# Two attention layers on one core: the last head group is normalised with its channels in rows, and the instruction lists are reordered

## The chip, the cores and the metric

The kernel runs on one core of a Trainium2 chip. The metric is the time of one execution on the device, in microseconds (us). TensorE (PE) multiplies and transposes, VectorE (DVE) and ScalarE (ACT) work on tiles, GpSimd (POOL) prepares tables and small tiles, SyncE (SP) issues DMAs. "Ln" is line n of the kernel.

## What is computed

A map `x` of 16 x 16 positions with 192 channels goes through two layers, each `x = x + attention(groupnorm(x))`:

```python
def _gn(v, G=32, eps=1e-05): ...           # mean and variance over positions and 6 channels
q, k, v = proj(x)                          # 12 heads of 16 channels, 256 tokens
attn = (q * scale) @ k.T                   # per head, 256 x 256
attn = attn + rel_h[..., :, None] + rel_w[..., None, :]   # from q and tables of 31 x 16
out = softmax(attn) @ v
return out @ wo + bo
```

The second layer adds low-rank parts to its q and v weights. Everything is float32.

## The kernel before, in words

The kernel is one hand-written list of instructions for each engine, with a semaphore wait ahead of every step that needs another engine's result. The order on an engine is the order of its list; no scheduler changes it. Both layers run the same lists. The 192 channels are held as two chunks of 96 rows; 12 heads are three groups (g) of four, or six pairs (p).

**Start.** SP loads `x`, then for each layer the input weights `win` and the output weights `wout` (three DMAs: 128 rows, 64 rows, the bias row). PE runs matmuls on a zero tile (`keep_busy`, L587) whose result nobody reads: 23 at the start, 3 between the two matmul groups that sum the statistics (`group_records`, L598 and L601), 12 before the projections of layer 0. DVE computes the statistics (L513, L517, L523), POOL the inverse deviation (L229), DVE the normalised input `xn` (L533).

**Projections and moves.** PE projects q and k (`project`, L785) and v (`values`, L775); ACT and DVE split q and k into a rounded and a rest part (`zq`, `zk`, `z_hi` and `z_lo`). `relative` (L804, four quarters) makes the position terms, which ACT rounds (`relative_rounded`) and DVE completes (`relative_rest`, L482). `key_rows` (L627), `query_rows` (L641) and `relative_rows` (L658) spread a group over PSUM banks, and 18 "moves" (`ACT_MOVES`, 12, and `DVE_MOVES`, 6; kind, group, odd or even heads) copy them to `ks` and `qs`. Kind k, q or r names which of the three it is. Group 0 and 1 share banks, so the spread of the next group waits for the moves of the one before it.

**Scores.** For each pair, `scores` (L672) makes scores with the queries in rows, DVE takes each row's maximum (`maxima`, L476), POOL splits it (`split_maxima`), PE turns it (`turn_max`, L686), ACT writes it beside the queries (`max_rows`). `scores_t` (L700) makes the scores again with the keys in rows, less the maximum, and ACT takes the exponential of a pair (`probabilities`, L382) or, for the last pair, of half a pair at a time (`last_probabilities`, L388). `max_rows` and `move` share one helper line, L335, on ACT.

**End of a layer.** `probs_v` (L719) multiplies the probabilities of a group by `va`, which holds for each head 16 value columns, a column of ones and 15 of zeros, so the product of a group has 128 rows: per head 16 channels, the softmax sum, 15 zeros. In each group it is copied to `ot` (DVE for groups 0 and 1, `out_columns`, L488; ACT for group 2), turned to tokens in rows (`turn_out`, L729), normalised by a reciprocal of the 8 sums of a row and a product (`normalise`, L467 and L469) into `on`, and turned back (`turn_on`, L736, first channels 0 to 127, then the remaining 64), and ACT copies each to `ont`. `residual` (L744, L749) puts `x` into the output banks and `output_product` (L757 in layer 0, L760 in layer 1) adds the product with `wout`: first both halves m of chunk 0, then both of chunk 1, whose extra row of ones brings the bias. In layer 0, DVE's next statistics wait for each half; in layer 1, ACT and DVE copy out the result and it is stored.

The list of PE at the end of a layer:

```python
scores_t(l, 4, 0); scores_t(l, 4, 1)
turn_out(l, 0)
scores_t(l, 5, 0); scores_t(l, 5, 1)
probs_v(l, 1); probs_v(l, 2)
turn_out(l, 1); residual(l, 1); turn_out(l, 2)
turn_on(l, 0); residual(l, 0); turn_on(l, 1)
```

Of the kernel before, what the change touches and what calls it, by code (L numbers as in the profile page):

```python
# [12 lines left out]
P = 128  # L13
# [20 lines left out]
def attention_layers(nc, x, w_in0, w_out0, w_in1, w_out1, lora, rel, out):  # L34
# [4 lines left out]
    with ctx:  # L39
# [3 lines left out]
        def sem(name):  # L43
# [52 lines left out]
        rinv = sb("rinv", [P, NG, TT, G4])  # L96
        on = sb("on", [P, TT, C])
# [32 lines left out]
        rstd_sb = sem("rstd_sb")  # L130
        lora_zero, lora_sb = sem("lora_zero"), sem("lora_sb")
# [11 lines left out]
        O_BANK, NM_BANK = [2, 2, 5], 3  # L143
        ONT_BANK = [3, 2]
# [10 lines left out]
        ON_ROWS = [P, C - P]  # L155
# [68 lines left out]
        def _(pool):  # L224
# [67 lines left out]
            pool.wait_ge(parts_hi, 1)  # L292
            spread_steps(0, 0)
# [39 lines left out]
        def _(act):  # L333
# [63 lines left out]
            for l in range(LAYERS):  # L397
# [37 lines left out]
        def _(dve):  # L435
# [3 lines left out]
            dve.memset(xn[CH:CH + 1, 0, :], 1.0).then_inc(made_ones, 1)  # L439
            dve.memset(ont[C - P:C - P + 1, 1, :], 1.0).then_inc(made_ones, 1)  # L440
            dve.memset(onehot[:, :, :], 0.0).then_inc(key_rows_sb, 1)
            dve.memset(pick_rh[:, :, 0:2].bitcast(F32), 0.0).then_inc(pick_zero, 1)
            dve.memset(pick_rh[:, :, 33:64].bitcast(F32), 0.0).then_inc(pick_zero, 1)
            dve.memset(pick_rl[:, :, 0:33].bitcast(F32), 0.0).then_inc(pick_zero, 1)
            dve.wait_ge(key_rows_sb, 1)
            dve.memset(onehot[64:66, :, :], 1.0).then_inc(key_rows_sb, 1)
            dve.wait_ge(made_ident, 1)
            dve.tensor_reduce(head_mask[:, :], ident[:, :].rearrange("p (s j c) -> p j s c", s=2, j=G4),
                              AX.XY, ALU.add).then_inc(made_mask, 1)
# [7 lines left out]

            def move(l, n):
# [4 lines left out]
            def normalise(l, g):  # L463

                dve.wait_ge(oq_ps, NG * l + g + 1)
                q = ps[:, O_BANK[g], T:2 * T].rearrange("p (t j d) -> p t j d", t=TT, j=G4)
                dve.reciprocal(rinv[:, g, :, :], q[:, :, :, D]).then_inc(ri_sb, 1)  # L467
                dve.wait_ge(ri_sb, NG * l + g + 1)
# [35 lines left out]
            for l in range(LAYERS):  # L504

                for ic in range(NC):
# [7 lines left out]
                    if l == 0 and ic == 0:  # L514
# [5 lines left out]
                                      ALU.mult).then_inc(spread_sb, 1)  # L520
                for ic in range(NC):
                    dve.wait_ge(gn_ps, NC * l + ic + 1)
                    dve.bn_aggr(mv[:, l, ic, :], ps[0:CH, GN_BANK[ic], 0:6 * GROUP]).then_inc(mv_sb, 1)  # L523
                    if l == 0 and ic == 0:
                        dve.wait_ge(rels_sb, 1)
                        dve.tensor_tensor(step[:, 0, :, :], *step_args(0), ALU.subtract).then_inc(step_sb, 1)
                dve.wait_ge(mv_sb, NC * l + NC)
# [29 lines left out]
                move(l, 0)  # L557
                move(l, 1)
                relative_rest(l, 0)
                relative_rest(l, 1)  # L560
                move(l, 2)
                relative_rest(l, 2)
# [9 lines left out]
                out_columns(l, 0)  # L572
                normalise(l, 0)
                out_columns(l, 1)
                normalise(l, 1)
                normalise(l, 2)
# [4 lines left out]
        def _(pe):  # L581
# [124 lines left out]
            def probs_v(l, g, tiles=range(TT)):  # L706
# [5 lines left out]
                elif g == 1:  # L712
                    pe.wait_ge(on_sb, NG * l + 1)
# [9 lines left out]
            def turn_out(l, g):  # L723
                if g < 2:
                    pe.wait_ge(ot_sb, 2 * l + g + 1)
                else:
                    pe.wait_ge(ot_act, l + 1)
# [5 lines left out]
            def turn_on(l, kc):  # L733
                pe.wait_ge(on_sb, NG * l + 2 + kc)
                for t in range(TT):
                    last = pe.transpose(ps[0:ON_ROWS[kc], ONT_BANK[kc], t * P:(t + 1) * P],  # L736
                                        on[:, t, kc * P:kc * P + ON_ROWS[kc]], ident[:, :])
# [15 lines left out]
            def output_product(l, kc, m):  # L753

                k = ON_ROWS[kc] + kc
                if l == 0:
                    return mm(ps[0:CH, Y_BANK + m, 0:T], wout[0][0:k, kc, m * CH:(m + 1) * CH],  # L757
# [180 lines left out]
```

## Time and profile before

| | |
|---|---|
| median of 3 runs | 73.58 us (73.19 to 73.86) |
| profiled execution | 74.05 us, of which the span is 72.3 us |
| PE busy | 65.3 us, 90% of the span |
| PE weight loads | 53.5 us, 74% |
| DVE | 48.4 us, 67% |
| ACT | 49.0 us, 68% |
| POOL | 26.5 us, 37% |

The span is the time from the first to the last recorded work. Busy time counts an instruction from its start to its end. Matmuls overlap, so that the distance between their starts, and not the mean duration, is what one costs in a row of them. Layer 0 fills the span to about 38 us, layer 1 the rest.

### The profile page before, as it was taken

To read this page: it belongs to the slowest core of one execution; us is meant where nothing else is said; L and a number is where in the kernel's file an instruction comes from. 1 tells how busy PE (TensorE), PEld (TensorE's weight loads), DVE (VectorE), ACT (ScalarE), POOL (GpSimd) and SP (SyncE) were. 2 spreads that over 40 slices of the span, in tenths; PEclk is the share of its full clock that TensorE was granted. 3 is DMA by queue.
4 is the path that set the end of the run, shared out by engine and by line. 5 is a ranking of instruction groups with operands and counts; after the bars stand their busy time and mean duration, and the time that the engine had idled before them with its cause. 6 is when DMAs were issued, how large, how long until landed. Compare 5 with 4: busy or idle time off the path is not lost.

```text
span 72.3 us, 1550 instructions
## 1 busy us (share of the span) xinstructions
PE 65.3 (90%) x564; PEld 53.5 (74%) x564; DVE 48.4 (67%) x110; ACT 49.0 (68%) x92; POOL 26.5 (37%) x61
## 2 busy tenths in 40 slices
PE   4999999999988999989999698999987998989960
PEld 4889779999965977664679587999956896655640
DVE  3886437899999898222518939899999897223410
ACT  3962056398999999995324057589999999994410
POOL 5755999997013222899901400000022223000000
PEclk9999999999999999999999999999999999999999
DMA  0978300000000000000000000000000000000003
GB/s 1 206 241 257 102 0 0 9 0 0 0 5 0 0 0 0 14 0 0 0 0 0 5 9 0 0 0 0 0 0 0 0 9 0 0 0 0 0 0 109
DMA packets 1575, 1.75 MB, mean 24 GB/s; under 512 B 344, under 2 KB 1178, under 8 KB 1568
## 3 DMA queue, kind: packets, MB, share of 16 engines
q1 hardware_dynamic: 1280, 1.49, 7.5%
q10 hardware_dynamic: 288, 0.16, 0.7%
q8 instruction: 4, 0.07, 0.4%
q14 instruction: 3, 0.02, 0.1%
HBM read 1.46 MB, written 0.20 MB: 23 GB/s over the span
## 4 chain that ended last, share of the span: by engine, by line
PE 62%; ACT 23%; DVE 7%; issue 3%
ACT pt L382 11%; PE ps L804 10%; ACT qs L335 10%; PE ps L785 9%; PE ps L587 6%; PE ps L672 5%; PE ps L719 5%; PE ps L775 3%; PE ps L641 3%; PE ps L658 3%; PE ps L757 3%; PE ps L627 2%; PE ps L760 2%; PE ps L736 2%; PE ps L700 2%
## 5 line engine op out<-in xcount | busy, mean ns | idle before, releaser
L335 ACT ACTIVATE qs<-ps 64x512 fp32r<-64x512 f32 (+1 forms) x30 | 17.7, 589 | 0.9
L476 DVE TENSOR_REDUCE nm<-ps 128x2 f32<-128x512 f32 x24 | 15.5, 687 | 1.2 <-PE ps L672 0.8
L315 POOL CAST nmhl<-nm 128x4 fp32r<-128x4 f32 x12 | 2.2, 187 | 27.0 <-DVE nm L476 27.0
L672 PE MATMUL ps<-ks,qs 128*128 128x256 f32 x48 | 10.4, 306 | 0.9 <-DVE nm L476 0.3
L382 ACT ACTIVATE pt<-ps 128x1024 f32<-128x1024 f32 x10 | 10.3, 1026 | 0.2
L700 PE MATMUL ps<-qs,ks 128*128 128x256 f32 x48 | 9.5, 300 | 0.8 <-ACT qs L335 0.8
L672 PEld LDWEIGHTS ps<-ks,qs 128*128 128x128 f32 x48 | 7.1, 189 | 2.8 <-issue 2.7
L785 PE MATMUL ps<-xn,win 97*128 97x256 f32 (+1 forms) x24 | 7.9, 496 | 0.6 <-DVE xn L533 0.6
L700 PEld LDWEIGHTS ps<-qs,ks 128*128 128x128 f32 x48 | 6.9, 189 | 1.7 <-issue 1.6
L785 PEld LDWEIGHTS ps<-xn,win 97*128 97x128 f32 (+1 forms) x24 | 6.1, 260 | 1.9 <-issue 0.7
L335 ACT ACTIVATE zq<-ps 64x256 fp32r<-64x256 f32 x6 | 2.3, 378 | 7.1 <-PE ps L785 6.9
L719 PE MATMUL ps<-pt,va 128*32 128x256 f32 x96 | 6.1, 384 | 0.0
L335 ACT ACTIVATE rr_hi<-ps 64x384 fp32r<-64x384 f32 x8 | 3.9, 483 | 3.2 <-PE ps L804 3.0
L587 PE MATMUL ps<-busy 128*128 128x128 bf16 x40 | 4.9, 308 | 1.1 <-DVE busy L438 1.1
L488 DVE COPY ot<-ps 128x256 f32<-128x256 f32 x4 | 1.7, 425 | 5.7 <-PE ps L719 5.7
L686 PE MATMUL ps<-ident_r,nmhl 128*2 128x128 f32 x48 | 4.8, 222 | 0.6 <-ACT qs L335 0.6
L587 PEld LDWEIGHTS ps<-busy 128*128 128x128 bf16 x40 | 4.3, 150 | 1.1 <-DVE busy L438 1.1
L555 DVE TENSOR_TENSOR zq<-ps,zq 64x256 fp32r<-64x256 f32 x6 | 2.5, 421 | 3.4 <-ACT zq L335 3.3
L804 PEld LDWEIGHTS ps<-zq,table_w 128*64 128x64 f32 x64 | 4.2, 138 | 0.5 <-DVE zq L555 0.5
L804 PE MATMUL ps<-zq,table_w 128*64 128x48 f32 x64 | 4.4, 218 | 0.2 <-DVE zq L555 0.2
L686 PEld LDWEIGHTS ps<-ident_r,nmhl 128*2 128x2 f32 x48 | 3.0, 83 | 2.1 <-ACT qs L335 1.9
L461 DVE CAST qs<-ps 64x512 fp32r<-64x512 f32 x6 | 4.1, 690 | 0.5 <-PE ps L641 0.4
(105 smaller groups left out, 126.4 us busy)
## 6 DMA issues: line engine op xcount, KB each, us to landing
win<-in_w_in_dram SPq DMA_DIRECT2D x4, 216.0 KB
xt<-in_x_dram SPq DMA_DIRECT2D x2, 96.0 KB, 2.3
wout<-in_w_out_dram SPq DMA_DIRECT2D x2, 96.0 KB
wout<-in_w_out_dram SPq DMA_DIRECT2D x2, 48.0 KB
out_dram<-res ACTq DMA_DIRECT2D x1, 96.0 KB, 1.7
out_dram<-res SPq DMA_DIRECT2D x1, 96.0 KB, 1.7
rel_raw<-in_rel_dram ACTq DMA_DIRECT2D x1, 62.0 KB, 2.5
win<-in_w_in_dram SPq DMA_DIRECT2D x2, 2.2 KB
```

What stands on the lines that cost most here:

```text
L335: return act.activation(dst, src, ACT.Copy, scale=scale)
L382: act.activation(pt[:, p, :, :, :].rearrange("p a k t -> p a (k t)"), ps[:, ST_BANK[p % 2]:ST_BANK[p % 2] + 2, :], ACT.Exp, scale=SCALE[l] ...
L461: dve.tensor_copy(dst, src).then_inc(moved_dve, 1)
L476: dve.tensor_reduce(nm[:, p, a, :], ps[:, S_BANK[a], :].rearrange("p (t k) -> p t k", k=T), AX.X, ALU.max, negate=True).then_inc(max_sb, 1)
L555: dve.tensor_tensor(z[64:P, g, :], chunk_rows(which, g), z[0:64, g, :].bitcast(F32), ALU.subtract).then_inc(z_lo, 1)
L587: mm(ps[:, bank, 0:P], busy[:, :], busy[:, :], start=True, stop=True)
L672: last = mm(ps[:, S_BANK[a], t * T:(t + 1) * T], qs[:, 2 * p + a, t * P:(t + 1) * P], ks[:, 2 * p + a, :], start=True, stop=True)
L686: last = mm(ps[0:2, NM_BANK, a * T + t * P:a * T + (t + 1) * P], nmhl[:, p, a, t, :], ident_r[:, :], start=True, stop=True)
L700: last = mm(ps[:, ST_BANK[p % 2] + a, t * T:(t + 1) * T], ks[:, 2 * p + a, t * P:(t + 1) * P], qs[:, 2 * p + a, :], start=True, stop=True)
L719: last = mm(ps[32 * j:32 * j + 32, O_BANK[g], 0:T], va[:, t, G4 * g + j, :], pt[:, 2 * g + j // 2, j % 2, t, :], start=(t == 0), stop=(t = ...
L785: last = mm(ps[:, m, 0:T], win[l][0:rows, ic, m * P:(m + 1) * P], xn[0:rows, ic, :], start=(ic == 0), stop=(ic == 1))
L804: last = mm(ps[0:64, b, c:c + NG * HW], rows.rearrange("p r j -> p (r j)"), moving, start=(part == 0), stop=(part == 1))
```

## The change

Groups 0 and 1 keep their way, but are turned back together in one `turn_on` (128 channels in rows). Group 2 isn't turned any more: ACT copies its 128 rows to `ot`, a product with a 0/1 matrix `sums_of` puts the sum of a head into each of its 32 rows (`last_sums`), and DVE takes the reciprocal of 128 x 256 sums and multiplies the group by it straight into chunk 1 of `ont` (`normalise_last`). The output weights are padded on the host to 256 rows to match: per head of group 2, 16 rows of weights and 16 of zeros, but for the bias in the row that belongs to the first head's sum. They come in one DMA for each layer.

Group 1's product gets the bank of the even heads' scores, so `probs_v(1)` waits for the maximum of the last pair's even head (before: for group 0's normalised tile) and is now ahead of the last pair's scores. The lists of moves, the early list of DVE, the PE order around scores and the numbers of filler matmuls change.

```diff
-        O_BANK, NM_BANK = [2, 2, 5], 3
-        ONT_BANK = [3, 2]
+        O_BANK, NM_BANK = [2, 4, 5], 3
+        ONT_BANK = 3
...
-        ACT_MOVES = [("k", 0, 0), ("k", 1, 0), ("q", 1, 0), ("q", 1, 1), ("r", 0, 0), ("r", 1, 1),
-                     ("q", 2, 1), ("r", 1, 0), ("q", 2, 0), ("r", 2, 0), ("r", 2, 1), ("k", 2, 1)]
-        DVE_MOVES = [("q", 0, 0), ("q", 0, 1), ("k", 0, 1), ("k", 1, 1), ("r", 0, 1), ("k", 2, 0)]
-
-        BUSY_AT_START = 23
-        BUSY_BETWEEN_RECORDS, BUSY_BEFORE_QK = [3, 0], [12, 2]
+        ACT_MOVES = [("q", 0, 0), ("k", 0, 0), ("k", 1, 1), ("q", 1, 1), ("k", 2, 1), ("r", 0, 0),
+                     ("r", 1, 0), ("q", 2, 0), ("r", 1, 1), ("q", 2, 1), ("k", 2, 0), ("r", 2, 0)]
+        DVE_MOVES = [("q", 0, 1), ("k", 0, 1), ("k", 1, 0), ("q", 1, 0), ("r", 0, 1), ("r", 2, 1)]
+
+        BUSY_AT_START = 28
+        BUSY_BETWEEN_RECORDS, BUSY_BEFORE_QK = [2, 0], [18, 2]
...
-                sp.dma_start(wout[l][:, 0, :], w_out[0:P, :]).then_inc(ld_wout[l], 16)
-                sp.dma_start(wout[l][0:C - P, 1, :], w_out[P:C, :]).then_inc(ld_wout[l], 16)
-                sp.dma_start(wout[l][C - P:C - P + 1, 1, :], w_out[C:C + 1, :]).then_inc(ld_wout[l], 16)
+                sp.dma_start(wout[l][:, :, :], w_out.rearrange("(k p) c -> p k c", p=P)).then_inc(ld_wout[l], 16)
...
             pool.wait_ge(parts_hi, 1)
+            pool.wait_ge(tab_w, 2)
             spread_steps(0, 0)
...
                 relative_rounded(l, 0)
+                move(l, 0)
                 relative_rounded(l, 1)
-                move(l, 0)
+                move(l, 1)
                 relative_rounded(l, 2)
-                move(l, 1)
+                move(l, 2)
                 relative_rounded(l, 3)
-                for n in range(2, 11):
+                for n in range(3, 11):
                     move(l, n)
...
-                for kc in range(2):
-                    act.wait_ge(ont_ps, 2 * l + kc + 1)
-                    copy(ont[0:ON_ROWS[kc], kc, :],
-                         ps[0:ON_ROWS[kc], ONT_BANK[kc], 0:T]).then_inc(ont_sb, 1)
+                act.wait_ge(ont_ps, l + 1)
+                copy(ont[:, 0, :], ps[:, ONT_BANK, 0:T]).then_inc(ont_sb, 1)
...
+            def masks():
+                dve.tensor_reduce(head_mask[:, :], ident[:, :].rearrange("p (s j c) -> p j s c", s=2, j=G4),
+                                  AX.XY, ALU.add).then_inc(made_mask, 1)
+
+            def pick_zeros():
+                dve.memset(pick_rh[:, :, 0:2].bitcast(F32), 0.0).then_inc(pick_zero, 1)
+                dve.memset(pick_rh[:, :, 33:64].bitcast(F32), 0.0).then_inc(pick_zero, 1)
+                dve.memset(pick_rl[:, :, 0:33].bitcast(F32), 0.0).then_inc(pick_zero, 1)
+                dve.tensor_copy(sums_of[:, :, :], ident[:, :].rearrange("p (j d) -> p j d", d=VW)[:, :, D:D + 1]
+                                .to_broadcast([P, G4, VW])).then_inc(made_sums_of, 1)
...
+            def normalise_last(l):
+
+                dve.wait_ge(sum_ps, l + 1)
+                dve.reciprocal(rsum[:, :], ps[:, O_BANK[2], T:2 * T]).then_inc(rsum_sb, 1)
+                dve.wait_ge(rsum_sb, l + 1)
+                dve.tensor_tensor(ont[:, 1, :], ps[:, O_BANK[2], 0:T], rsum[:, :], ALU.mult).then_inc(ont_dve, 1)
...
+            def last_sums(l):
+
+                pe.wait_ge(made_sums_of, 1)
+                pe.wait_ge(ot_act, l + 1)
+                mm(ps[:, O_BANK[2], T:2 * T], sums_of[:, :, :].rearrange("p j d -> p (j d)"), ot[:, 2, :],
+                   start=True, stop=True).then_inc(sum_ps, 1)
```

On DVE, `masks()` moves from the early list to behind the two `spread` steps of layer 0, and `pick_zeros()` from the early list to behind the two L523; the memset of a row of `ont` is gone. The moves and rests of DVE become move 0, rest 0, move 1, rest 1, rest 2, move 2, rest 3, moves 3 and 4, values. On PE:

```diff
                 relative(l, 3)
+                values(l, 0, 1)
                 query_rows(l, 1)
-                values(l, 0, 1)
                 values(l, 1, 0)
+                key_rows(l, 2)
                 relative_rows(l, 0, 0)
                 relative_rows(l, 0, 1)
                 relative_rows(l, 1, 0)
+                values(l, 1, 1)
                 relative_rows(l, 1, 1)
-                values(l, 1, 1)
+                scores(l, 0, 0)
                 query_rows(l, 2)
-                scores(l, 0, 0)
+                scores(l, 0, 1)
+                scores(l, 1, 0)
                 relative_rows(l, 2, 0)
-                scores(l, 0, 1)
-                relative_rows(l, 2, 1)
-                scores(l, 1, 0)
                 scores(l, 1, 1)
-                key_rows(l, 2)
                 scores(l, 2, 0)
                 turn_max(l, 0)
+                relative_rows(l, 2, 1)
                 scores(l, 2, 1)
...
                 scores_t(l, 4, 1)
+                probs_v(l, 1)
+                scores_t(l, 5, 0)
                 turn_out(l, 0)
-                scores_t(l, 5, 0)
                 scores_t(l, 5, 1)
-                probs_v(l, 1)
+                turn_out(l, 1)
                 probs_v(l, 2)
-                turn_out(l, 1)
+                turn_on(l)
                 residual(l, 1)
-                turn_out(l, 2)
-                turn_on(l, 0)
+                last_sums(l)
                 residual(l, 0)
-                turn_on(l, 1)
```

## Rows read from the trace of the kernel before

**Rows 1.** Chain that ended last, in order of time: start us, us, what
```profile
1.05 2.63 PE ps L587 x23
...
5.80 1.28 PE ps L587 x12
7.08 4.84 PE ps L785 x12
...
20.02 0.70 DVE nm L476
...
22.68 0.26 PE ps L686 x4
...
22.96 0.58 ACT qs L335
...
30.82 0.59 ACT qs L335
...
31.55 0.71 PE ps L700 x4
32.26 1.90 PE ps L719 x32
...
36.25 1.85 PE ps L757 x8
...
40.79 1.55 PE ps L785 x6
```

**Rows 2.** Page, 40 slices of the span: TensorE clock granted, in tenths
```profile
PEclk9999999999999999999999999999999999999999
```

**Rows 3.** Timeline of the start: start us, us, engine, line, tiles
```profile
0.81 0.84 SPq L165 DMA_DIRECT2D xt<-in_x_dram  x2
...
3.58 0.42 DVE L513 BATCH_NORM_STATS2 stats<-xt 96x6 f32<-96x256 f32 x1
...
3.81 0.51 PE L598 MATMUL ps<-eps_records,group 96*96 96x36 f32 x2
...
6.19 0.41 DVE L533 TENSOR_SCALAR xn<-xt,mv,rstd 96x256 f32<-96x256 f32 x1
```

**Rows 4.** Page, DMA issues: KB each, median us from issue to landing
```profile
xt<-in_x_dram SPq DMA_DIRECT2D x2, 96.0 KB, 2.3
```

**Rows 5.** Timeline from the moves to the first scores, ACT
```profile
14.40 0.48 ACT L335 ACTIVATE rr_hi<-ps 64x384 fp32r<-64x384 f32 x1 [0.74 <-PE ps L804]
...
17.33 6.21 ACT L335 ACTIVATE qs<-ps 64x512 fp32r<-64x512 f32 x10
```

**Rows 6.** Timeline of the end of layer 0
```profile
30.93 0.38 PE L729 MATMUL ps<-ident,ot 128*128 128x128 f32 x2
...
31.43 1.02 ACT L382 ACTIVATE pt<-ps 128x1024 f32<-128x1024 f32 x1
...
32.35 1.08 ACT L388 ACTIVATE pt<-ps 128x512 f32<-128x512 f32 x2
...
34.22 0.38 ACT L335 ACTIVATE ot<-ps 128x256 f32<-128x256 f32 x1 [0.78 <-PE ps L719]
...
35.43 0.60 PE L744 MATMUL ps<-xt,ident 96*96 96x256 f32 x2
...
37.70 0.43 DVE L513 BATCH_NORM_STATS2 stats<-ps 96x6 f32<-96x256 f32 x1 [1.95 <-PE ps L757]
```

**Rows 7.** Groups of DVE instructions by shape: count | busy us, mean ns
```profile
L461 DVE CAST qs<-ps 64x512 fp32r<-64x512 f32 x6 | 4.1, 690 | 0.5 <-PE ps L641 0.4
...
L488 DVE COPY ot<-ps 128x256 f32<-128x256 f32 x4 | 1.7, 425 | 5.7 <-PE ps L719 5.7
...
L467 DVE RECIPROCAL rinv<-ps 128x8 f32<-128x8 f32 x6 | 1.2, 208 | 3.0 <-PE ps L729 2.9
...
L578 DVE COPY res<-ps 128x192 f32<-128x192 f32 x1 | 0.4, 357 | 2.1 <-PE ps L760 2.1
```

**Rows 8.** Timeline of the end of layer 1
```profile
68.28 1.54 PE L760 MATMUL ps<-wout,ont 128*128 128x192 f32 x8
```

More of the change, by code:

```diff
@@ L95, in attention_layers @@
         ot = sb("ot", [P, NG, T])
-        rinv = sb("rinv", [P, NG, TT, G4])
-        on = sb("on", [P, TT, C])
+        sums_of = sb("sums_of", [P, G4, VW])
+        rsum = sb("rsum", [P, T])
+        rinv = sb("rinv", [P, NG - 1, TT, G4])
+        on = sb("on", [P, TT, P])
         ont = sb("ont", [P, 2, T])
@@ L130, in attention_layers @@
         rstd_sb = sem("rstd_sb")
+        made_sums_of, sum_ps, rsum_sb, ont_dve = (sem(n) for n in ("made_sums_of", "sum_ps", "rsum_sb", "ont_dve"))
         lora_zero, lora_sb = sem("lora_zero"), sem("lora_sb")
@@ L438, in _ @@
             dve.memset(busy[:, :], 0.0).then_inc(made_busy, 1)
-            dve.memset(xn[CH:CH + 1, 0, :], 1.0).then_inc(made_ones, 1)
-            dve.memset(ont[C - P:C - P + 1, 1, :], 1.0).then_inc(made_ones, 1)
             dve.memset(onehot[:, :, :], 0.0).then_inc(key_rows_sb, 1)
-            dve.memset(pick_rh[:, :, 0:2].bitcast(F32), 0.0).then_inc(pick_zero, 1)
-            dve.memset(pick_rh[:, :, 33:64].bitcast(F32), 0.0).then_inc(pick_zero, 1)
-            dve.memset(pick_rl[:, :, 0:33].bitcast(F32), 0.0).then_inc(pick_zero, 1)
             dve.wait_ge(key_rows_sb, 1)
             dve.memset(onehot[64:66, :, :], 1.0).then_inc(key_rows_sb, 1)
+            dve.memset(xn[CH:CH + 1, 0, :], 1.0).then_inc(made_ones, 1)
             dve.wait_ge(made_ident, 1)
-            dve.tensor_reduce(head_mask[:, :], ident[:, :].rearrange("p (s j c) -> p j s c", s=2, j=G4),
-                              AX.XY, ALU.add).then_inc(made_mask, 1)
             dve.tensor_reduce(member[:, :], ident[0:CH, 0:CH].rearrange("p (g k) -> p k g", k=GROUP),
@@ L520, in _ @@
                                       ALU.mult).then_inc(spread_sb, 1)
+                if l == 0:
+                    masks()
                 for ic in range(NC):
@@ L526, in _ @@
                         dve.tensor_tensor(step[:, 0, :, :], *step_args(0), ALU.subtract).then_inc(step_sb, 1)
+                if l == 0:
+                    pick_zeros()
                 dve.wait_ge(mv_sb, NC * l + NC)
@@ L557, in _ @@
                 move(l, 0)
+                relative_rest(l, 0)
                 move(l, 1)
-                relative_rest(l, 0)
                 relative_rest(l, 1)
+                relative_rest(l, 2)
                 move(l, 2)
-                relative_rest(l, 2)
                 relative_rest(l, 3)
@@ L572, in _ @@
                 out_columns(l, 0)
+                out_columns(l, 1)
                 normalise(l, 0)
-                out_columns(l, 1)
                 normalise(l, 1)
-                normalise(l, 2)
+                normalise_last(l)
             dve.wait_ge(y_ps, NC + 2)
@@ L712, in probs_v @@
                 elif g == 1:
-                    pe.wait_ge(on_sb, NG * l + 1)
+                    pe.wait_ge(max_sb, NH * l + NH - 1)
                 else:
@@ L723, in turn_out @@
             def turn_out(l, g):
[L724 to L727, printed above, removed]
+                pe.wait_ge(ot_sb, 2 * l + g + 1)
                 for t in range(TT):
@@ L731, in turn_out, with turn_on @@
                 last.then_inc(oq_ps, 1)
-            def turn_on(l, kc):
-                pe.wait_ge(on_sb, NG * l + 2 + kc)
+            def last_sums(l):
[3 more added lines that the diff above has]
+                   start=True, stop=True).then_inc(sum_ps, 1)
+            def turn_on(l):
+                pe.wait_ge(on_sb, 2 * l + 2)
                 for t in range(TT):
-                    last = pe.transpose(ps[0:ON_ROWS[kc], ONT_BANK[kc], t * P:(t + 1) * P],
-                                        on[:, t, kc * P:kc * P + ON_ROWS[kc]], ident[:, :])
+                    last = pe.transpose(ps[:, ONT_BANK, t * P:(t + 1) * P], on[:, t, :], ident[:, :])
                 last.then_inc(ont_ps, 1)
@@ L753, in output_product @@
             def output_product(l, kc, m):
-                k = ON_ROWS[kc] + kc
                 if l == 0:
-                    return mm(ps[0:CH, Y_BANK + m, 0:T], wout[0][0:k, kc, m * CH:(m + 1) * CH],
-                              ont[0:k, kc, :], start=False, stop=(kc == 1), skip_group_check=True)
-                return mm(ps[:, Y_BANK + m, 0:C], ont[0:k, kc, m * P:(m + 1) * P],
-                          wout[1][0:k, kc, :], start=False, stop=(kc == 1), skip_group_check=True)
+                    return mm(ps[0:CH, Y_BANK + m, 0:T], wout[0][:, kc, m * CH:(m + 1) * CH],
+                              ont[:, kc, :], start=False, stop=(kc == 1), skip_group_check=True)
+                return mm(ps[:, Y_BANK + m, 0:C], ont[:, kc, m * P:(m + 1) * P],
+                          wout[1][:, kc, :], start=False, stop=(kc == 1), skip_group_check=True)
             def lora_columns(s):
@@ L814, in _ @@
                 keep_busy(BUSY_BEFORE_QK[l])
[L816 removed]
+                pe.wait_ge(made_ones, 1)
                 pe.wait_ge(ld_win[l], 48)
@@ L864, in _ @@
                 scores_t(l, 1, 0)
+                scores_t(l, 1, 1)
                 scores(l, 4, 0)
-                scores_t(l, 1, 1)
                 scores(l, 4, 1)
@@ L911, in with_bias, with out_rows @@
         return _np.insert(weights, row, bias, axis=0)
+    def out_rows(weights, bias):
+        last = _np.zeros((G4, VW, C), weights.dtype)
+        last[:, 0:D, :] = weights[P:C].reshape(G4, D, C)
+        last[0, D, :] = bias
+        return _np.concatenate([weights[0:P], last.reshape(P, C)], axis=0)
     def columns(rel):
```

16 lines of the change are left out of this document (7 added, 9 removed).

## The prediction

> **What bounds the kernel now.** I read the chain of waits first [rows 1]. It hands over between engines: PE up to the first maxima (20.02), DVE and PE to the first turned maximum (22.68), ACT from 22.96 to 31.42, then PE, with short steps of DVE and ACT, to the end of the layer. Layer 1 repeats this 32.1 us later. Since every stage has its own bound, I go by stage and not by busy shares.
>
> At the start PE runs at half its clock, though the slices say that the full one is granted throughout [rows 2]. A filler of 128 columns costs 1.28 / 12 = 0.107 us, which is 1.2 GHz. The 12 passes of L785 in layer 0 cost 4.84 / 12 = 0.40 us, in layer 1 1.55 / 6 = 0.26 us, waits included [rows 1]. So the rise to 2.4 GHz comes only at the end of those passes, near 11.4 us.
>
> **The start.** DVE's early list is shorter by the memset of `ont`, the masks and the pick zeros, so the first L513, at 3.58, can begin when its `x` lands: issue at 0.81 plus 2.3 us is about 3.15 [rows 3, 4], a gain of 0.4 us. But 28 fillers end at 1.05 + 28 x 0.107 = 4.05, and the record sums stand behind them on PE. Before, they began at 3.81 [rows 3]. The 0.4 us are spent, and the last record sum ends some 0.1 us earlier, at 5.7, by the filler that is gone between them. Then 18 fillers (1.93 us) instead of 12 (1.28): PE is ready for L785 at 7.43 instead of 6.87. On DVE `masks` falls into a wait. `pick_zeros` (three memsets and a copy, about 0.5 us) stands ahead of `xn`, which moves from 6.19 [rows 3] to 6.6, and its second half from 6.8 to 7.0; both are there before 7.43. The price is 0.56 us at 1.2 GHz. If the clock rises at the same 11.4, the passes left over run twice as fast, and 0.3 us remains. I take 0.33, with 0 to 0.6 as bounds. POOL's key rows and tables shift by 0.2 to 0.3 us; their readers come over a microsecond later. Two DMAs fewer per layer on SP bring the second layer's weights earlier; nothing waits for them, and the padded output weights, a third larger, are read at 36 us.
>
> **The moves.** Before, ACT has gaps while `relative` runs (0.74 us ahead of 14.40) and none from 17.33 on [rows 5]. The new list puts a third move into such a gap, worth 0.6 us of ACT. But the stage ends with the turned maximum at 22.93, and that follows from DVE: first maximum at 20.02, the third 2.1 us later, the pair 2 scores, the turn. DVE's work ahead of its first maximum is the same five moves (0.69 us each [rows 7]), four rests and the values, with nearly no idle time. Only their order is new. Walked through with these durations, the first maximum starts at 20.07, the first turned maximum ends at 22.95, and the 0.6 us of ACT become idle time while it waits for it. From there ACT has the same list. I take 0 for each layer, bounds -0.3 and +0.3.
>
> **The last pair.** PE used to idle until ACT had written the last maximum (30.82 + 0.59), then made L700 in 0.71 us, ended at 32.26, and ACT's halves could start at 32.35 on time, behind the exponential of 31.43 + 1.02 [rows 1, 6]. Now `probs_v(1)` fills the idle time: 32 passes cost 1.90, so 16 cost about 0.9, from 30.93 [rows 6] to 31.82. Behind it stand `scores_t(5, 0)` 0.24 (about half of 0.71 less the same end), `turn_out(0)` 0.22 (0.38 in its row, less 0.16 in which its last pass only comes out), `scores_t(5, 1)` 0.24 plus 0.16 until its result is out: 32.68. ACT's two halves wait for this and end at 33.80 instead of 33.43. The new wait of `probs_v(1)`, for the even maximum of pair 5, is met before that, since ACT writes the turned maxima of the pair at 30.82; behind it on PE stand `scores_t(5)` and all that ends the layer. Against this, PE has less to do behind: the last 8 passes now wait for ACT alone, and end at 34.47 instead of 34.17. A loss of 0.3 us per layer here.
>
> **Group 2.** Then, in layer 0, with each step from the rows of before:
> - ACT copies `ot` in 0.38 [rows 6]: 34.53 to 34.91. In the meantime PE makes `turn_on` (0.22) and `residual(1)` (0.43: 0.60 in its row less its end), ready at 34.92.
> - `last_sums`: two passes over 256 columns, 0.43, result at 35.54. Its nearest rows are the passes of L757: 1.85 / 8 = 0.23 each.
> - `residual(0)` to 35.82, `output_product(0, 0 and 1)` to 36.68. Its operand `ont` 0 comes from ACT at 35.31, no wait.
> - The reciprocal of 128 x 256 from 35.60, then a product of 0.43 like a copy of this size [rows 7].
> - `output_product(1, 0)` 0.22 plus 0.38 until out, then the next layer's L513, before at 37.70 [rows 6].
>
> No row shows a wide reciprocal. DVE's copies from PSUM cost 0.357, 0.425 and 0.690 us for 192, 256 and 512 elements, 1.04 ns for each more. By that line a copy of 8 elements would cost 0.166; the reciprocal of 8 costs 0.208 [rows 7]. The extra 0.042 us is either fixed, and then the wide one costs 0.425 + 0.042 = 0.47 us; or it comes with each element, 5.2 ns, and then the wide one costs 0.425 + 256 x 0.0052 = 1.77 us. I take the second: the two bounds are a factor of four apart, the only row with this operation lies off the line of the copies, and what is off grows with the elements as soon as any part of it belongs to them. It is an inference from one point, and its chance below says so.
>
> The Trainium skill ("VectorE: DVE Perf Modes", section "First, the fixed hardware budget") says that `Reciprocal` is an iterative divide on slices 0 and 1 "with a repeat count of 8". If that were 8 cycles of 0.96 GHz for each element, an estimate from this page is 2.3 us for 256, and the sum would be 1.0 us higher. The row for 8 elements speaks for fewer, about 6.
>
> So the reciprocal ends at 37.37, the product at 37.82, the output product is out at 38.46, against 37.68 before: +0.78 in layer 0. Turned around, with 0.47 us the product is done at 36.5, before PE is, and the result is out at 37.28: -0.40. The work removed (a turn of `ot` 0.22, one of `on` 0.22, on DVE 0.21 + 0.29, on ACT a copy of 0.38) is what pays for this.
>
> Layer 1 is the same 32.1 us later but for a residual on 96 columns (0.17 for 0.43, an estimate by size) and passes of 192 columns, 1.54 / 8 = 0.19 with the end [rows 8]. `last_sums` is out at 67.66, the reciprocal at 69.49, the product at 69.93, and the first half of the output at 70.46 instead of 69.5: +0.95. With 0.47 us it would be 69.14, -0.37, since PE, done with chunk 0 at 68.33, is then bound by little.
>
> Sum: 0.33 + 0 + 0.78 + 0.95 = +2.06 us, from 74.05 to 76.1 in a profiled execution. That one lies 0.47 above the median of 73.58; I carry the difference over: 75.6 us, 2.8% slower.
>
> **Rivals.**
> - **The wide reciprocal is cheap (0.47 us).** For it: a fixed cost of 0.04 us fits the row for 8 elements as well. Then 0.33 - 0.40 - 0.37 = -0.44, 73.1 us. It decides at about 0.6 us, below which PE reaches chunk 1 only after DVE's product in layer 0; at 0.8 us gain and loss cancel. This is the case on the other side, not slower.
> - **The clock rises before the projection.** For it: 3.0 us of unbroken filler instead of 2.4, and again 1.9 before L785; against it: 10 us of nearly unbroken matmuls didn't raise it before. The 12 passes would cost 0.26 as in layer 1 and not 0.40 [rows 1], 12 x 0.14 = 1.7; less 0.56 of filler that is a gain of 1.1, or 1.2 with the record sums' 0.1: 74.4 with the slow reciprocal, 71.9 with the cheap one. The Trainium skill ("TensorE: Matmul & The Clock Gate", Part 1) says that activity releases the clock; it would make this rival more likely than the row does.
> - **The stage of the moves gets shorter by the 0.6 us that ACT saves** in each layer, since DVE isn't what sets its end: 74.4 with the slow reciprocal. Against it: by the walk above, DVE's list up to its first maximum is as long as before.
>
> **How the numbers follow.** Slow reciprocal as forecast 0.55, cheap 0.30, early clock 0.12 (0.07 slow, 0.05 with the cheap one), shorter moves 0.03. A measurement here can't tell less than about 1%. Faster than 72.8: 0.13 of the cheap case, 0.05 of early clock, 0.01: 0.19. Slower than 74.3: 0.54 of the forecast, 0.02 of early clock, 0.02: 0.58. Within: 0.23. The forecast's own range is 74.8 to 76.4, from a reciprocal of 1.6 to 2.0 and a start of 0 to 0.6. To hold 8 in 10, the range reaches down over most of the cheap case, to 72.7.
>
> **What the profile after would show.** The new reciprocal on 128 x 256 as a row of DVE: near 1.8 us or near 0.5. PE idle ahead of the last `output_product` in both layers, released by DVE's write of `ont`. ACT's L388 starting about 0.4 us later behind the last L382, released by PE. L785 starting near 7.4 and its passes at 0.43 us until about 11.4. The first L476 near 20.4. The prediction is wrong if the reciprocal has the price of a copy, or if the clock rises earlier.

## The result: 1.6% slower

The changed kernel takes 74.87 us (median of 4 runs, 74.44 to 75.57), the kernel before 73.59 in the same session. The ratio is 1.016, 95% interval 1.009 to 1.023. The profiled execution took 74.78 us with a span of 72.9, against 74.05 and 72.3.

The new instruction first: groups of DVE instructions by shape, of the changed kernel.

```profile
L481 DVE RECIPROCAL rsum<-ps 128x256 f32<-128x256 f32 x2 | 3.5, 1758 | 4.7 <-PE ps L750 4.7
L500 DVE COPY ot<-ps 128x256 f32<-128x256 f32 x4 | 1.7, 425 | 5.3 <-PE ps L735 5.3
...
L483 DVE TENSOR_TENSOR ont<-ps,rsum 128x256 f32<-128x256 f32 x2 | 0.8, 425 | 0.1
...
L472 DVE RECIPROCAL rinv<-ps 128x8 f32<-128x8 f32 x4 | 0.8, 208 | 0.4 <-PE ps L742 0.4
```

A copy of 128 x 256 takes 0.425 us, the reciprocal 1.758. The chain of waits of the changed kernel shows where that lies: start us, us, what.

```profile
2.64 3.82 DMA win<-in_w_in_dram
...
6.55 1.55 PE ps L803 x6
...
30.78 0.61 ACT pt L389
...
31.52 1.07 PE ps L735 x16
...
33.40 0.47 PE ps L750 x2
...
33.89 1.77 DVE rsum L481
...
35.68 0.43 DVE ont L483
...
36.16 1.10 PE ps L775 x4
...
66.58 0.68 PE ps L750 x2
...
67.28 1.77 DVE rsum L481
...
69.08 0.44 DVE ont L483
...
69.56 0.93 PE ps L778 x4
```

Before, no division stood in this chain at the end of layer 0, which PE held from L719 to L757 [rows 1]. Now DVE holds it for 2.2 us in each layer, and PE is idle ahead of the second half of `output_product`. The timeline of the changed kernel shows the two idle times that are new, ahead of ACT's last exponentials and ahead of that product.

```profile
29.77 0.51 PE L716 MATMUL ps<-qs,ks 128*128 128x256 f32 x2
29.91 0.43 DVE L500 COPY ot<-ps 128x256 f32<-128x256 f32 x1 [1.42 <-PE ps L735]
30.11 0.38 PE L742 MATMUL ps<-ident,ot 128*128 128x128 f32 x2
...
30.25 0.49 PE L716 MATMUL ps<-qs,ks 128*128 128x256 f32 x2
...
30.78 1.09 ACT L389 ACTIVATE pt<-ps 128x512 f32<-128x512 f32 x2 [0.57 <-PE ps L716]
...
36.16 1.10 PE L775 MATMUL ps<-ont,wout 128*96 128x256 f32 x4 [1.01 <-DVE ont L483]
...
36.87 0.43 DVE L525 BATCH_NORM_STATS2 stats<-ps 96x6 f32<-96x256 f32 x1 [0.76 <-PE ps L775]
```

L389 waits 0.57 us for PE's `scores_t` of the last pair; its counterpart L388 in [rows 6] waits for nothing. The L525 there answers to L513 at 37.70 [rows 6].

At the start it went the other way. Timeline of the changed kernel:

```profile
1.06 3.12 PE L603 MATMUL ps<-busy 128*128 128x128 bf16 x28 [1.06 <-DVE busy L438]
...
3.12 0.42 DVE L525 BATCH_NORM_STATS2 stats<-xt 96x6 f32<-96x256 f32 x1 [0.29 <-DMA xt<-in_x_dram]
...
4.76 1.17 PE L603 MATMUL ps<-busy 128*128 128x128 bf16 x18
...
5.66 0.93 DVE L549 TENSOR_SCALAR xn<-xt,mv,rstd 96x256 f32<-96x256 f32 x2
...
6.55 2.83 PE L803 MATMUL ps<-xn,win 97*128 97x256 f32 x12 [0.62 <-DMA win<-in_w_in_dram]
```

18 fillers in 1.17 us with the last one's end are some 0.06 apiece, half of the 0.107 of before: the clock was at 2.4 GHz before 4.76. The 12 projection passes took 2.83 us; before, they were in the chain for 4.84 [rows 1]. The column of the granted clock says 1.0 in both [rows 2], since the trace has no record of the low stretch: its first record of the clock begins at 3.99 us in the changed kernel and at 11.40 in the kernel before. What lies ahead of that is shown only by the distance between matmuls.

Cutting the profiled executions at the same instructions gives each change its place. Microseconds between the starts of: the first L785 (L803), the first `relative`, the first exponential of the layer (L382), the first half of the last pair's (L388), the next layer's L513 or, in layer 1, the last copy (L578). The first column counts from the span's start.

```
                       L785   ->rel  ->L382 ->L388 ->L513 | ->L382 ->L388 ->L578   last copy at
before                 6.87   5.08   12.84  7.56   5.35   | 19.22  7.56   5.38     69.86
changed                6.55   3.36   12.64  8.23   6.09   | 19.08  8.23   6.33     70.51
copy_for_recip         6.91   3.35   12.62  8.23   4.84   | 19.07  8.22   5.00     68.24
order_old_probs        6.53   3.36   12.64  7.56   6.08   | 19.08  7.56   6.32     69.13
probs_behind           6.82   3.36   12.63  7.56   7.40   | 19.07  7.56   7.64     72.04
old_last_group         6.67   3.36   12.63  7.56   5.35   | 19.09  7.56   5.38     67.60
lists_and_new_tail     6.90   3.37   12.64  7.79   6.07   | 19.08  7.80   5.75     69.40
```

The stages behind the first `relative` are steady to 0.02 us across kernels that share them; only the first `L382` of the kernel before stands alone, 0.07 later than the 12.77 of four other kernels with its lists. Changed against before: start -2.04, lists -0.20 and -0.14, `probs_v(1)` ahead of the last scores +0.67 twice, the way of group 2 +0.74 and +0.95; in all +0.65. The ratios leave out the executions that took over 1.5% more than the fastest of their kernel; some were disturbed by the chip (up to 84 us), but others only raised PE's clock late, and the section on the clock counts these.

### The profile page after: what moved, and what is told of

The parts are those of the page before. It is cut to its first block, busy times and chain, and to the rows that moved or that the text cites. A ratio compares the mean times of both kernels' runs of the same rounds, so it can differ in the third digit from the quotient of the medians.

```text
span 72.9 us, 1560 instructions
## 1 busy us (share of the span) xinstructions
PE 61.8 (85%) x570; PEld 50.9 (70%) x570; DVE 51.7 (71%) x110; ACT 48.4 (66%) x90; POOL 26.6 (37%) x61
## 4 chain that ended last, share of the span: by engine, by line
PE 64%; DVE 12%; ACT 9%; DMA 5%; issue 4%; SPq 2%
PE ps L822 10%; PE ps L716 9%; PE ps L735 8%; PE ps L688 8%; ACT qs L336 7%; DMA win<-in_w_in_dram 5%; DVE rsum L481 5%; PE ps L702 5%; PE ps L803 4%; DVE zq L571 3%; PE ps L793 3%; PE ps L674 3%; PE ps L643 2%; PE ps L657 2%; ACT pt L389 2%
## 5 line engine op out<-in xcount | busy, mean ns | idle before, releaser
L336 ACT ACTIVATE qs<-ps 64x512 fp32r<-64x512 f32 (+1 forms) x28 | 16.3, 589 | 2.1 <-PE ps L657 1.0
L716 PE MATMUL ps<-qs,ks 128*128 128x256 f32 x48 | 9.5, 299 | 0.0
L716 PEld LDWEIGHTS ps<-qs,ks 128*128 128x128 f32 x48 | 6.8, 189 | 1.0 <-issue 0.8
L481 DVE RECIPROCAL rsum<-ps 128x256 f32<-128x256 f32 x2 | 3.5, 1758 | 4.7 <-PE ps L750 4.7
L803 PE MATMUL ps<-xn,win 97*128 97x256 f32 (+1 forms) x24 | 5.7, 385 | 1.2 <-DMA win<-in_w_in_dram 0.6
L466 DVE CAST qs<-ps 64x512 fp32r<-64x512 f32 x8 | 5.5, 689 | 0.4 <-PE ps L657 0.3
L803 PEld LDWEIGHTS ps<-xn,win 97*128 97x128 f32 (+1 forms) x24 | 4.4, 189 | 2.0 <-issue 1.5
L702 PE MATMUL ps<-ident_r,nmhl 128*2 128x128 f32 x48 | 4.8, 222 | 0.3 <-ACT qs L336 0.3
L336 ACT ACTIVATE ks<-ps 64x512 fp32r<-64x512 f32 x8 | 4.8, 594 | 0.1
```

What stands on the lines that cost most here:

```text
L336: return act.activation(dst, src, ACT.Copy, scale=scale)
L466: dve.tensor_copy(dst, src).then_inc(moved_dve, 1)
L481: dve.reciprocal(rsum[:, :], ps[:, O_BANK[2], T:2 * T]).then_inc(rsum_sb, 1)
L702: last = mm(ps[0:2, NM_BANK, a * T + t * P:a * T + (t + 1) * P], nmhl[:, p, a, t, :], ident_r[:, :], start=True, stop=True)
L716: last = mm(ps[:, ST_BANK[p % 2] + a, t * T:(t + 1) * T], ks[:, 2 * p + a, t * P:(t + 1) * P], qs[:, 2 * p + a, :], start=True, stop=True)
L803: last = mm(ps[:, m, 0:T], win[l][0:rows, ic, m * P:(m + 1) * P], xn[0:rows, ic, :], start=(ic == 0), stop=(ic == 1))
```

## The experiments

Each was timed beside the kernel before on the same chip; ratios are to that.

**Is it the reciprocal?** `copy_for_recip` leaves the division out: group 2 is multiplied by its sums.

```diff
-                dve.reciprocal(rsum[:, :], ps[:, O_BANK[2], T:2 * T]).then_inc(rsum_sb, 1)
+                dve.tensor_copy(rsum[:, :], ps[:, O_BANK[2], T:2 * T]).then_inc(rsum_sb, 1)
```

> The changed kernel, but the wide reciprocal of group 2 (128 x 256, twice) is a copy of the same size, so that the last group is multiplied by its sums and not divided. Theory: the reciprocal's 1.76 us stand on the path in both layers; a copy takes 0.43. In layer 0 PE then reaches chunk 1 at about 34.98 instead of 36.16 (bound by its own chunk 0), in layer 1 at 68.2 instead of 69.56: 2.5 us less than the changed kernel, about 72.3 us. Rival: the tail is bound by something that the wide reciprocal only covers (ACT's copies, the sums), and the time stays above 74.

Measured: 72.34 us, ratio 0.982 (0.975 to 0.988). From the end of layer 0 in its timeline:

```profile
34.22 0.42 DVE L481 COPY rsum<-ps 128x256 f32<-128x256 f32 x1 [2.35 <-PE ps L750]
34.45 1.89 PE L775 MATMUL ps<-ont,wout 128*96 128x256 f32 x8
34.68 0.42 DVE L483 TENSOR_TENSOR ont<-ps,rsum 128x256 f32<-128x256 f32 x1
```

PE's 8 passes of L775 run through, without the idle time. The stage to L513 falls from 6.09 to 4.84, that to L578 from 6.33 to 5.00: 1.25 and 1.33, where the instruction itself is 1.33 shorter. Against the old way (5.35 and 5.38) the new one would have been 0.51 and 0.38 shorter. So the way of group 2 was sound but for the price of one instruction. The changed kernel as a whole wasn't: the 0.67 ahead of it in each layer stays, and 72.34 us is no less than the kernel before reaches with 28 fillers at the start alone (72.09, below).

**Is it the place of `probs_v(1)`?** Two tries to put it back behind the last scores.

```diff
 # probs_behind
-                probs_v(l, 1)
                 scores_t(l, 5, 0)
-                turn_out(l, 0)
                 scores_t(l, 5, 1)
+                turn_out(l, 0)
+                probs_v(l, 1)
                 turn_out(l, 1)
                 probs_v(l, 2)
```

> The changed kernel with probs_v(1) behind both scores_t of the last pair again. Theory: ACT's last exponentials start 0.5 us earlier in each layer, behind the fifth pair's without a gap; PE then has 16 passes more between them and the end of group 2, so that only 0.2 to 0.3 us of it is left: 0.5 us less in all, about 74.4 us. Rival: the gap costs nothing, since PE's passes are the bound either way, within 0.1 us of 74.9.

Measured: 76.62 us, ratio 1.039 (1.032 to 1.045), 1.7 us more than the changed kernel. The gap ahead of L389 is gone (7.56), but the stage behind it is 1.31 longer in each layer, and the timeline shows a worse gap there.

```profile
30.43 1.07 PE L735 MATMUL ps<-pt,va 128*32 128x256 f32 x16
31.57 0.42 DVE L500 COPY ot<-ps 128x256 f32<-128x256 f32 x1 [2.83 <-PE ps L735]
...
32.05 0.44 PE L742 MATMUL ps<-ident,ot 128*128 128x128 f32 x2 [0.55 <-DVE ot L500]
...
32.41 0.59 PEld L735 LDWEIGHTS ps<-pt,va 128*32 128x32 f32 x16 [0.17 <-issue]
32.41 1.07 PE L735 MATMUL ps<-pt,va 128*32 128x256 f32 x16
```

`turn_out(1)` needs DVE's copy of the product that PE has just made, and all 16 passes of `probs_v(2)` stand behind that wait. Neither my expectation nor its rival had counted that wait. The second try takes `turn_out(1)` behind `probs_v(2)` as in the kernel before, and the sums ahead of the turn of chunk 0.

```diff
 # order_old_probs
-                probs_v(l, 1)
+                turn_out(l, 0)
                 scores_t(l, 5, 0)
-                turn_out(l, 0)
                 scores_t(l, 5, 1)
-                turn_out(l, 1)
+                probs_v(l, 1)
                 probs_v(l, 2)
-                turn_on(l)
+                turn_out(l, 1)
                 residual(l, 1)
                 last_sums(l)
+                turn_on(l)
```

> The changed kernel with turn_out(0), both scores_t(5), probs_v(1), probs_v(2), turn_out(1), residual(1), last_sums, turn_on in this order: the last exponentials don't wait for PE, and the sums are made before chunk 0 is turned. Group 2 keeps its wide reciprocal. Theory: the sums are done 0.7 us earlier in each layer, 1.5 us less in all, 73.4 us. Rival: as when probs_v(1) alone was put back, PE waits for DVE's copy instead and the time stays at 74.9 or more.

Measured: 73.73 us, ratio 1.007 (1.003 to 1.011). The 0.67 comes back whole in both layers. The rest of the expected 1.5 doesn't: L481 starts 3.10 us after L389 (3.11 in the changed kernel), since the sums now stand behind 16 more passes.

```profile
29.93 1.97 PE L735 MATMUL ps<-pt,va 128*32 128x256 f32 x32
30.09 1.08 ACT L389 ACTIVATE pt<-ps 128x512 f32<-128x512 f32 x2
...
32.54 0.61 PE L750 MATMUL ps<-ot,sums_of 128*128 128x256 f32 x2
...
33.19 1.76 DVE L481 RECIPROCAL rsum<-ps 128x256 f32<-128x256 f32 x1 [0.35 <-PE ps L750]
```

**What is left with the old end of a layer?** `old_last_group` takes the end of a layer, the output weights' DMAs and 192 rows from the kernel before, the rest from the changed one (its memset of the row of ones goes with `pick_zeros`). `wout_late` also loads the output weights last.

```diff
 # old_last_group
-                probs_v(l, 1)
-                scores_t(l, 5, 0)
-                turn_out(l, 0)
-                scores_t(l, 5, 1)
...
+                turn_out(l, 0)
+                scores_t(l, 5, 0)
+                scores_t(l, 5, 1)
+                probs_v(l, 1)
+                probs_v(l, 2)
                 turn_out(l, 1)
...
 # wout_late, on top of it
+            for l, w_out in enumerate((w_out0, w_out1)):
                 sp.dma_start(wout[l][:, 0, :], w_out[0:P, :]).then_inc(ld_wout[l], 16)
```

> The changed kernel with the end of a layer of before: group 2 turned and normalised with tokens in rows, 192 output rows, the old order from probs_v(0) on, the old order of DVE's last steps. Fillers, moves, early list and PE order up to there are the changed kernel's. Theory: the way of group 2 and its order cost 1.27 us in layer 0 and 1.47 us in layer 1 by the two profiles, and taking them out gives 74.87 - 2.7 = 72.1 us, the same as the kernel before with the new fillers alone (72.07), since the new lists of moves are worth nothing. Rival: the new lists are worth 0.5 us or more: 71.6 us or less.

> As old_last_group, with the output weights of both layers loaded after the input weights of both. With the clock up early, the first projection waited 0.6 us for its weights in the changed kernel. Theory: the output weights share the DMA engines with them, and without them the weights of layer 0 land about 0.4 us earlier: 0.3 to 0.4 us less than old_last_group. Rival: the landing is set by the weights' own descriptors, or the fillers stand ahead anyway: the same time.

Measured: `old_last_group` 72.73 us, ratio 0.989 (0.983 to 0.995), 0.6 above the theory; six of its eleven executions took 71.86 (the profiled one) to 72.73, the others 73.0 to 75.1. `wout_late` took 72.22, ratio 0.987 (0.982 to 0.992). The table gives `old_last_group` the two end stages of before in each layer (7.56, then 5.35 and 5.38) and the 12.63 and 19.09 of the new lists. So the lists are worth 0.13 to 0.2 us in each layer by the stages, too little for these times to tell. It isn't 0.5 us better than the new fillers alone (0.979, below), so the rival, that the new lists are worth that, falls. `wout_late` didn't tell: its interval overlaps, and the projection of `old_last_group` didn't wait for its weights in the first place.

```profile
6.67 2.83 PE L795 MATMUL ps<-xn,win 97*128 97x256 f32 x12 [0.78 <-DVE xn L543]
```

**What raised the clock?** The filler counts alone, in both directions:

```diff
 # before_new_filler: in the kernel before, all three; start_filler_only: the first; qk_filler_only: the 18
 # after_old_filler and old_filler_again: in the changed kernel, all three back
-        BUSY_AT_START = 23
-        BUSY_BETWEEN_RECORDS, BUSY_BEFORE_QK = [3, 0], [12, 2]
+        BUSY_AT_START = 28
+        BUSY_BETWEEN_RECORDS, BUSY_BEFORE_QK = [2, 0], [18, 2]
```

The moments in the expectations are the first records of the granted clock in the traces.

> The kernel before with the filler counts of the changed one (28, 2, 18). Theory A, the filler decides when the clock rises: it rises near 4 us, the first projection runs at the full clock, 1.5 us less than before, about 72.1 us. Theory B: the fillers only push the projection back, 0 to 0.6 us more than before, 73.6 to 74.2 us.

Measured: 72.07 us, ratio 0.979 (0.971 to 0.986), from four of seven executions.

> The kernel before with 28 fillers at the start for 23, the other two counts as before. Theory A, the unbroken run at the start is what raises the clock: it rises near 4 to 6 us, and without the 6 fillers before the projection the time is at most that of all new counts, 71.8 to 72.1 us. Theory B, the 18 before the projection matter: 73.6 us.

Measured: 72.09 us, ratio 0.978 (0.975 to 0.982), from four of six.

> The kernel before with 18 fillers ahead of the first projection for 12, the other counts as before. Theory A: the clock rises late, and six more fillers at 0.107 us cost 0.3 us, 73.9 us. Theory B: the clock rises before the projection, 72.1 us.

Measured: 74.28 us. The ratio of 1.000 (0.994 to 1.006) rests on only three of twelve executions (73.05, 73.21 and 74.11); six more took 74.24 to 74.34 and lie just outside it.

> The changed kernel with the filler counts of before (23, 3, 12 for 28, 2, 18). Theory A, the filler raised the clock early (3.99 us into the span for 11.40): here it rises late again, L803 of layer 0 costs 0.43 a pass, and the time is 1.5 to 2 us more, about 76.6 us. Theory B, the early rise was chance or comes from the shorter early list of DVE: the time stays within 0.5 us of the changed kernel.

Measured: 74.78, 76.96 (profiled) and 77.36 us, and three from 82.5 to 84.4; no ratio. Repeated:

> The changed kernel with the filler counts of before, on another chip, since the first attempt had hardly any undisturbed run. Theory: the clock rises later than with the new counts in most executions: 0.5 to 1.5 us more than the changed kernel, 75.4 to 76.4 us. Rival: what raised the clock is the earlier statistics on DVE, and the time stays within 0.3 us of 74.9.

Measured: 75.41 us, ratio 1.019 (1.012 to 1.026). Three of its six runs took 74.4 to 74.8, as the changed kernel does, and three took 76.0 to 76.5.

The profiled executions of `old_filler_again` and `qk_filler_only` at the start:

```profile
5.11 1.47 PE L603 MATMUL ps<-busy 128*128 128x128 bf16 x12
6.50 4.08 PE L803 MATMUL ps<-xn,win 97*128 97x256 f32 x12
```

```profile
5.61 2.11 PE L587 MATMUL ps<-busy 128*128 128x128 bf16 x18
7.51 3.15 PE L785 MATMUL ps<-xn,win 97*128 97x256 f32 x12
```

In both the fillers ran at 1.2 GHz (1.47 us for 12 and 2.11 for 18, 0.107 apiece with the last one's end) and the clock rose during the projection. The profiled execution of `start_filler_only`, 73.38 us and so not one of its four short ones, did the same in spite of its 28 fillers:

```profile
5.60 1.47 PE L587 MATMUL ps<-busy 128*128 128x128 bf16 x12
...
6.87 3.96 PE L785 MATMUL ps<-xn,win 97*128 97x256 f32 x12
```

So the first record of the clock, and all executions, have to be set side by side. The fillers are those at the start, between the sums and ahead of the projection; `relative` is the start of the first one, from the span's start; `filler_and_new_tail` and `lists_and_new_tail` follow below and differ from each other at the start in DVE's early list and the order of the weights' DMAs.

```
                     fillers    DVE list  clock  relative | executions, us
before               23, 3, 12  old       11.40  11.95    | 23 of 29 at 72.98 to 74.06, 6 from 76.0
qk_filler_only       23, 3, 18  old        8.18  11.18    | 73.05, 73.21, 7 at 74.1 to 74.3, 3 at 81.2
start_filler_only    28, 3, 12  old        9.18  11.36    | 4 at 71.9 to 72.1, 73.38, 80.64
before_new_filler    28, 2, 18  old       10.41  12.11    | 4 at 71.9 to 72.1, 73.80, 74.12, 74.57
filler_and_new_tail  28, 2, 18  old        9.64  11.86    | 4 at 73.5 to 73.9, 8 at 75.5 to 76.9
after_old_filler     23, 3, 12  short      8.65  10.93    | 74.78, 76.96, 77.36, 3 from 82.5
old_filler_again     23, 3, 12  short      9.03  11.11    | 3 at 74.4 to 74.8, 3 at 76.0 to 76.5
changed              28, 2, 18  short      3.99   9.91    | 4 at 74.4 to 75.6
old_last_group       28, 2, 18  short      3.76  10.03    | 6 at 71.9 to 72.7, 73.00, 73.58, 74.12, 74.14, 75.06
lists_and_new_tail   28, 2, 18  short      4.60  10.27    | 11 at 73.5 to 74.0, 75.09
```

Five more fillers at the start let the kernel before reach 72.0 us, 1.5 less than its median, which none of its own 29 executions did; the three counts together bring no more, and the six ahead of the projection alone bring nothing. But the five don't secure it. With DVE's old list all three profiled executions with 28 fillers rose late (9.18 to 10.41), and only 4 of 6, 4 of 7 and 4 of 12 executions are of the shorter kind. With DVE's short list and 28 fillers all seven profiled ones rose early (3.76 to 6.43), and in the same session `lists_and_new_tail` has 11 of 12 where `filler_and_new_tail` has 4 of 12. Even so it isn't every time, if the longer five of `old_last_group` are late rises. The short list without the five fillers gives half: three of the six executions of `old_filler_again` take the time of the changed kernel. So both rivals hold in part: each change makes the early rise more frequent, and the ratios of 0.979 and 0.978 say what an early rise is worth, not what five fillers bring on average. That the short executions with the old list are early rises is inferred from their times, since none of them was profiled. What else moves the moment is open.

**A better end of a layer?** With the old way of group 2, half of `probs_v(1)` in PE's idle time ahead of the last scores, and PE's small work pulled forward:

```diff
 # filler_and_new_tail (on before_new_filler), lists_and_new_tail (on wout_late)
                 turn_out(l, 0)
+                probs_v(l, 1, [0])
                 scores_t(l, 5, 0)
                 scores_t(l, 5, 1)
-                probs_v(l, 1)
-                probs_v(l, 2)
-                turn_out(l, 1)
+                probs_v(l, 1, [1])
                 residual(l, 1)
-                turn_out(l, 2)
-                turn_on(l, 0)
+                probs_v(l, 2, [0])
+                turn_out(l, 1)
+                probs_v(l, 2, [1])
                 residual(l, 0)
-                turn_on(l, 1)
+                turn_on(l, 0)
+                turn_out(l, 2)
...
-                for m in range(2):
-                    output_product(l, 0, m)
+                output_product(l, 0, 0)
+                turn_on(l, 1)
+                output_product(l, 0, 1)
```

> The kernel before with the new filler counts and another order at the end of a layer, with group 2 in tokens as before: half of probs_v(1) goes into PE's idle time before the last scores_t (group 1's product gets bank 4 for this), residual(1) and turn_out(1) go ahead of the halves of probs_v(2), residual(0) and turn_on(0) ahead of turn_out(2), and turn_on(1) between the two products of chunk 0. Theory: PE has 0.4 us less behind the last exponentials and nothing in the way of group 2: 0.5 us less per layer than the new fillers alone (72.07), 71.1 us. Rival: the chain through ACT's and DVE's copies of group 2 is as long as before, and the time stays at 72.0.

> The same end of a layer on top of wout_late (the changed kernel's moves, early list and score order; output weights last). Theory: 1.0 us less than wout_late (72.22), 71.2 us, and equal to filler_and_new_tail, since the new lists are worth nothing. Rival: the new lists are worth 0.3 us or more on one of the two sides.

Measured: `filler_and_new_tail` 75.64 us, the median of all twelve; its ratio of 1.004 (0.998 to 1.010) is that of the four with an early rise (73.5 to 73.9). `lists_and_new_tail` 73.97 us, ratio 1.003 (0.999 to 1.006). By the ratios both are slower than what they stand on, by 2.6 and 1.6%. By the table `lists_and_new_tail` loses 0.23 us in each layer ahead of the last exponentials, and 0.72 and 0.37 behind them. Its timeline:

```profile
30.60 0.64 PE L730 MATMUL ps<-pt,va 128*32 128x256 f32 x8
30.70 1.08 ACT L390 ACTIVATE pt<-ps 128x512 f32<-128x512 f32 x2
31.16 0.67 PE L756 MATMUL ps<-xt,ident 96*96 96x256 f32 x2
...
31.77 0.64 PE L730 MATMUL ps<-pt,va 128*32 128x256 f32 x8
32.34 0.44 PE L741 MATMUL ps<-ident,ot 128*128 128x128 f32 x2
32.70 0.64 PE L730 MATMUL ps<-pt,va 128*32 128x256 f32 x8
...
33.41 0.38 ACT L337 ACTIVATE ot<-ps 128x256 f32<-128x256 f32 x1 [1.62 <-PE ps L730]
```

ACT had finished at 31.78, and the last 8 passes began at 32.70. PE and not ACT was the bound there: `residual(1)` (31.16 to 31.77) and `turn_out(1)` (32.34 to 32.70), 0.97 us by the distance between starts, stand ahead of the only passes that group 2 waits for.

## Why the prediction was right, and where it missed

**The reciprocal**, taken at 1.77 us from an excess of 0.042 us over 8 elements, measured 1.758. The other bound, a fixed excess and 0.47 us, is refuted, and with it the cheap rival. Between 8 and 256 elements it costs (1.758 - 0.208) / 248 = 6.25 ns an element, and carried back to none, 0.158 us: the same start as a copy. That the time hangs on this is shown by `copy_for_recip`. The repeat count of 8 in the Trainium skill ("VectorE: DVE Perf Modes", section "First, the fixed hardware budget"), read as 8 cycles an element, gave an estimate of 2.3 us. The row disagrees: 6.25 ns is 6 cycles of 0.96 GHz.

**The way of group 2** was right in mechanism and slightly low. The totals of +0.78 and +0.95 are made up of 0.37 for the later start of the last exponentials and 0.41 and 0.58 behind it; the stages say +0.74 and +0.95 behind it. The sums were ready 1.27 us after `probs_v(2)` in place of 1.07 in layer 0.

**The last pair** was taken at 0.37 us for ACT, of which 0.3 would arrive. It measured 0.67, and all of it arrived: `order_old_probs` gets it back, with the stage behind as long as in the changed kernel (6.08 for 6.09). That order differs in the place of the sums too, so how PE's shorter list behind was to save the 0.07 isn't tested apart. The term that was too small is the way through PE. The 16 passes took 1.00 us, where 0.89 was their share of a long row. The full-width matmuls behind them took 0.97 for 0.86 (29.77 to 30.74), and the last 0.07 lies ahead of them, where PE goes over from L716 to the 32-column passes.

**The moves** were put at 0 for each layer, bounds of 0.3. The stages say -0.20 and -0.14. The reasoning on the turned maximum held: its matmuls (L702, formerly L686) start 10.51 us after the first `relative`, where they started after 10.57. What is gained lies behind it.

**The start** is the step that failed: "if the clock rises at the same 11.4", +0.33. The first `relative` came 2.04 us earlier instead, with the clock at 2.4 GHz from 3.99 us. By the prediction's last sentence an earlier rise of the clock means that it is wrong, and so its mechanism was wrong here although its number and its sign hold. The second rival had this, with the slow reciprocal at 74.4 us, and a chance of 0.07. Its sum left in the 0.33 of the late clock; without it, it is 74.1. I held against it that 10 us of nearly unbroken matmuls hadn't raised the clock. The runs show that the moment isn't a property of the kernel alone: five fillers and the shorter list on DVE make an early one frequent. The price of "0.56 us at 1.2 GHz" for more filler was not paid either: at 2.4 GHz, 18 take little more than half the time, and they ended before the weights were there.

So 75.6 was 0.7 above the measured 74.87. About 2.4 us too much for the start, 0.3 for the moves, and 1.3 too little for the ends of the two layers make 1.4 by the two profiled executions; by medians it is half of that, since the profiled one of before, with its late clock, lay 0.47 above its median and the changed one's did not. The sign came from the reciprocal; that the size came out so near is luck, since errors of 2.4 and 1.3 us cancel in part.

The experiments favour small versions. The kernel before with 28 fillers at the start takes 72.09 us, 2.2% less than before and 3.7% less than the changed one, but not in every execution. `wout_late`, the changed kernel with the old end of a layer and the output weights loaded last, takes 72.22 and had all six executions between 71.88 and 72.47.

## What to carry to other kernels

A row on few elements can carry the price of a wide instruction: take the line of the copies away from it, and ask what the rest would be if it came with every element. Before a wide elementwise instruction goes on the path, that is worth one measured kernel, since here the same design gained 0.38 to 0.51 us or lost 0.74 to 0.95 us behind the last exponentials of a layer by it alone. And in front of a hand-over, count what stands on the engine that makes it: three reorderings filled PE's idle time or pulled small work forward, and each delayed the passes that others waited for. Where the times of one kernel fall into two groups, profile one of each before calling either a disturbance: here the longer group was a late clock, and the median of the shorter one says nothing of how often it comes.

## What the runs showed of the hardware

- DVE's reciprocal costs 6.25 ns an element beyond a start of 0.16 us (0.208 us for 128 x 8, 1.758 for 128 x 256), six times the copy's 1.04.
- The start of PE's full clock moved by over 7 us (from 11.40 to 3.99) with five small matmuls more at the start and a shorter list on DVE; the granted-clock column showed 1.0 all along. It also differs between executions of one kernel: those of `old_filler_again` fall at 74.4 to 74.8 and at 76.0 to 76.5 us. The time that this is worth is 1.5 to 2 us of 73.6.
- 16 passes in 32-column tiles took 1.00 us between other matmuls; 32 in a row took 1.90 with their end, the last 8 of them after a wait for ACT.
